# Two-layer graph network on 64 graphs: the layer-norm statistics of x, one pair of loads and the order of the first two graphs are moved

## What is computed

```python
h = relu(layernorm(x))                       # layer 0
q, k, v = h @ Wq.T + bq, h @ Wk.T + bk, h @ Wv.T + bv
w = adj * exp(q @ k.T)
x = x + (w / w.sum(axis=2)) @ v
h = relu(layernorm(x))                       # layer 1
A = adj + I; d = A.sum(-1) ** -0.5
x = x + (A * d[:, None] * d[None, :]) @ (h @ W + b)
```

## Time and profile before

| | us |
|---|---|
| median of 3 runs | 1716.59 (1712.29 to 1718.35) |
| the profiled execution | 1706.24 |
| its span, first to last instruction | 1704.4 |
| TensorE busy | 1640.7 (96%) |
| VectorE / ScalarE / GpSimd busy | 1475.4 / 1060.4 / 831.3 |

### The profile page before, as it was taken

How to read it: one execution, slowest core, us unless ns; L and a number is a source line. 1 busy time by engine, 2 the same in 40 slices (tenths; PEclk the granted TensorE clock), 3 DMA queues, 4 the chain that set the end, 5 groups by cost and what they waited for, 6 DMA issues and landing times.

```text
span 1704.4 us, 37784 instructions
## 1 busy us (share of the span) xinstructions
PE 1640.7 (96%) x12010; PEld 1551.3 (91%) x12010; DVE 1475.4 (87%) x3366; ACT 1060.4 (62%) x2451; POOL 831.3 (49%) x968
## 2 busy tenths in 40 slices
PE   8899999999999999999999999999999999999997
PEld 6798999999999999999998989999999999999996
DVE  5788888888888889888898889898888898888885
ACT  5656666666666666666666666666666666566552
POOL 2445445545545545545454554554554554454551
PEclk9899999999999999999999999999999999999998
DMA  5354554544544544544544544544544544545530
GB/s 171 83 146 116 124 136 118 131 132 114 139 130 118 137 126 122 137 123 121 142 122 112 148 117 117 149 120 116 151 117 117 149 120 116 146 117 122 145 100 28
DMA packets 494415, 212.66 MB, mean 125 GB/s; under 512 B 402496, under 2 KB 427072, under 8 KB 494400
## 3 DMA queue, kind: packets, MB, share of 16 engines
q1 hardware_dynamic: 492480, 210.89, 47.2%
q10 hardware_dynamic: 1920, 1.58, 0.3%
HBM read 146.28 MB, written 66.13 MB: 125 GB/s over the span
## 4 chain that ended last, share of the span: by engine, by line
DMA 28%; DVE 24%; issue 16%; SPq 14%; ACT 11%; PE 5%; POOL 1%; DVEq 0%; ACTq 0%; POOLq 0%
DMA x_in<-in_x_dram 15%; DMA h_scratch<-h 12%; SPq L185 10%; ACT unused_x L424 5%; ACT unused_x L431 5%; DVE z_lo L773 4%; DVE late L824 3%; DVE ht_lo L804 3%; DVE unused_a L793 3%; DVE p L784 3%; DVE p_lo L692 2%; DVE neg_mean L648 2%; SPq L223 2%; PE ps L836 2%; DVE v_lo L638 1%
## 5 line engine op out<-in xcount | busy, mean ns | idle before, releaser
L836 PE MATMUL ps<-ht_hi,m_hi 128*128 128x256 f32 x1024 | 287.2, 280 | 0.6 <-DVE m_lo L558 0.6
L838 PE MATMUL ps<-ht_lo,m_hi 128*128 128x256 f32 x1024 | 286.8, 280 | 0.0
L839 PE MATMUL ps<-ht_hi,m_lo 128*128 128x256 f32 x1024 | 286.4, 280 | 0.0
L408 ACT ACTIVATE g_hi<-ps,u_col 128x256 fp32r<-128x256 f32 x256 | 105.8, 464 | 251.8 <-PE ps L839 251.8
L284 POOL TENSOR_TENSOR ht_sum<-ht 128x256 f32<-128x256 f32 x64 | 47.4, 741 | 422.8 <-DVE ht L666 401.5
L836 PE MATMUL ps<-w_hi,z_hi 128*128 128x512 f32 x512 | 206.7, 404 | 38.1 <-DVE z_lo L773 38.1
L839 PE MATMUL ps<-w_hi,z_lo 128*128 128x512 f32 x512 | 202.0, 395 | 0.0
L838 PE MATMUL ps<-w_lo,z_hi 128*128 128x512 f32 x512 | 202.0, 394 | 0.0
L836 PEld LDWEIGHTS ps<-ht_hi,m_hi 128*128 128x128 f32 x1024 | 193.5, 189 | 0.7 <-DVE m_lo L558 0.7
L839 PEld LDWEIGHTS ps<-ht_hi,m_lo 128*128 128x128 f32 x1024 | 193.4, 189 | 0.0
L838 PEld LDWEIGHTS ps<-ht_lo,m_hi 128*128 128x128 f32 x1024 | 193.3, 189 | 0.0
(11 more groups left out here) (147 smaller groups left out, 5843.3 us busy)
## 6 DMA issues: line engine op xcount, KB each, us to landing
x_in<-in_x_dram SPq DMA_DIRECT2D x64, 512.0 KB, 4.3
xb<-in_x_dram SPq DMA_DIRECT2D x64, 512.0 KB, 4.9
out_dram<-late SPq DMA_DIRECT2D x128, 256.0 KB, 2.1
h_scratch<-h SPq DMA_DIRECT2D x62, 512.0 KB, 3.5
h_blocks<-h_scratch SPq DMA_DIRECT2D x248, 128.0 KB, 3.6
adj_in<-in_adj_dram SPq DMA_DIRECT2D x64, 256.0 KB, 2.9
adj_blocks<-in_adj_dram SPq DMA_DIRECT2D x256, 64.0 KB, 2.4
dn_row<-dn_scratch SPq DMA_DIRECT2D x64, 128.0 KB, 2.9
```

Source lines behind the costliest of these rows:

```text
L408: last = act.activation(g_hi[:, m, :], ps[:, G + j, m % 2 * N:m % 2 * N + N], ACT.Identity, bias=u_col[:, m:m + 1])
L836: pe.matmul(dst, a_hi[:, c, cols], b_hi[:, c, :], start=(first and c == 0), stop=False, skip_group_check=not first)
L838: pe.matmul(dst, a_hi[:, c, cols], b_lo[:, c, :], start=False, stop=False, skip_group_check=not first)
L839: end = pe.matmul(dst, a_lo[:, c, cols], b_hi[:, c, :], start=False, stop=(c == chunks - 1), skip_group_check=not first)
```

## The change

It moves work between places in the engines' orders; nothing of the computation is dropped.

- **Loop, statistics**: ACT runs `x_sums` between the two exponentials and `x_squares` after them. DVE runs `x_mean` between the two `p`, `x_variance` after the row sums of layer 1 and `x_shift` after `p_lo`. POOL's power for `rs_x` follows `ht_sum`.
- **Loop, rest**: SP loads `xb` ahead of `x_in`. POOL adds the bias to `xb` ahead of `ht_sum`, and makes `ht_sum_lo` ahead of `hat_lo`. On ACT `ht_sum_hi` and the adjacency's copy move behind `h` of the next step.
- **First two graphs**: `ht_lo` reads PSUM and not `ht`; the columns of `wt` come first and `values` waits for the parts of `wt_lo` one by one; the high and low part of W, the adjacency's copy and the statistics of graphs 2 and 3 move; TensorE waits for `ht_lo` where it waited for `ht`.

```diff
@@ sync: step
-                if second:
-                    x_second = x_flat[bass.ds(sp.snap((this + 1) * (N * D)), N * D)]
-                    if not prev:
-                        sp.wait_ge(h_ready[0], this + 1)
-                        sp.wait_ge(h_ready[1], this + 1)
-                    sp.dma_start(x_in[:], ...).then_inc(x_loaded, 16)
                 if main and prev:
                     ...
                     sp.dma_start(xb[:], ...).then_inc(xb_loaded, 16)
+                if second and prev:
+                    load_x(this)
...
+                if second and not prev:
+                    sp.wait_ge(h_ready[0], this + 1)
+                    sp.wait_ge(h_ready[1], this + 1)
+                    load_x(this)
@@ gpsimd: step
+                    if main:
+                        ht_sums_low(this)
                     pool.wait_ge(hat_hi_ready, this - 1)
...
-                    if main:
-                        ht_sums_low(this)
...
-                if main and ahead and prev:
-                    pool.wait_ge(v_done[V3], this)
-                    ht_sums(this + 1)
-                if second:
-                    pool.wait_ge(ve_x_done, this + 2)
-                    pool.tensor_tensor(rs_x[:], ve_x[:], minus_half[:], ALU.pow).then_inc(rs_x_done, 1)
                 if main:
                     ... (xb plus bias)
-                if main and ahead and not prev:
+                if main and not prev:
+                    x_power(this + 1)
+                if main and ahead:
                     pool.wait_ge(v_done[V3], this)
                     ht_sums(this + 1)
+                if second and main:
+                    x_power(this + 2)
@@ scalar: step
-                if main and ahead:
+                if main and ahead and prev:
                     layer_norm_x(this, prev, older)
+                if main and prev:
+                    ht_sums_high(this)
+                    keep_adjacency(this, True)
...
-                    if second:
-                        x_sums(this + 2)
+                    if not prev:
+                        x_sums(this + 1)
                     act.wait_ge(v_done[V2], this)
                     act.activation(v_hi[:, 0, 0, 0:HD], ps[:, VA, 0:HD], ACT.Copy).then_inc(v_hi_ready[0], 1)
-                    if second:
-                        x_squares(this + 2)
+                    if not prev:
+                        x_squares(this + 1)
...
                     for t in range(NT):
-                        if ahead and prev and t:
-                            ht_sums_high(this + 1)
+                        if t and not prev:
+                            layer_norm_x(this, prev, older)
+                        if t and second and prev:
+                            x_sums(this + 2)
                         ... (exponential t)
+                    if second and prev:
+                        x_squares(this + 2)
@@ vector: step
                     value_u3(this)
-                    if second:
-                        x_mean(this + 2)
                     value_sums(this)
                     value_low(this)
-                    if second:
-                        x_variance(this + 2)
...
-                    if second:
-                        x_shift(this + 2)
                     for t in range(NT):
+                        if t and second and prev:
+                            x_mean(this + 2)
                         ... (p of half t)
...
                 if main and prev:
+                    if second:
+                        x_variance(this + 2)
                     p_low(this)
+                    if second:
+                        x_shift(this + 2)
...
-                                          ht[:, 2 * j:2 * j + 2, :].rearrange("p c n -> p (c n)"),
+                                          ht[:, 2 * j:2 * j + 2, :].rearrange("p c n -> p (c n)") if prev
+                                          else ps[:, HT + j, :],
@@ tensor: values (weights_ready(2) to (8) in turn), step
-                weights_ready(8)
+                weights_ready(2)
                 value(V1, VA, ht_rows(0), upper, B11, HD + 2)
                 pe.wait_ge(ht_sum_lo_ready, 2 * this)
+                weights_ready(3)
                 value(V6, VB, sums(S2), whole, T2, HD + 2)
...
                         if ahead and not prev and t:
-                            pe.wait_ge(ht_ready[0], this + 1)
-                            pe.wait_ge(ht_ready[1], this + 1)
+                            pe.wait_ge(ht_lo_ready[0], this + 1)
+                            pe.wait_ge(ht_lo_ready[1], this + 1)
```

More of the change, by code:

```diff
@@ L217, in _, with load_x @@
             adj_flat, x_flat = adj.rearrange("g n m -> (g n m)"), x.rearrange("g n d -> (g n d)")
+            def load_x(this):
+                x_second = x_flat[bass.ds(sp.snap((this + 1) * (N * D)), N * D)]
+                sp.dma_start(x_in[:], x_second.rearrange("(t p d) -> p t d", p=P, d=D)).then_inc(x_loaded, 16)
             def step(this, prev, main, ahead, older=True, second=True):
@@ L433, in x_squares, with keep_adjacency @@
                 last.then_inc(x_square_ready, 1)
+            def keep_adjacency(graph, main=False):
+                act.wait_ge(adj_loaded, graph * 16)
+                if main:
+                    act.wait_ge(sd_ready, graph - 1)
+                for t in range(NT):
+                    last = act.activation(adj_kept[:, t, :], adj_in[:, t, :], ACT.Copy,
+                                          accum_out=rsum[:, t:t + 1])
+                last.then_inc(rsum_ready, 1)
             def hat_high(this):
@@ L473, in step @@
                     layer_norm_x(this, prev, older)
+                    keep_adjacency(this + 1)
                     for j in range(2):
@@ L482, in step @@
                     wt_high()
-                    x_sums(this + 2)
-                    x_squares(this + 2)
+                    w_high()
                 if prev:
@@ L514, in step @@
                                        ACT.Copy).then_inc(ht_hi_ready[j], 1)
[L515 to L524, removed]
                 if main and not prev:
-                    w_high()
+                    x_sums(this + 2)
+                    x_squares(this + 2)
             steps(act, step)
@@ L584, in wt_low @@
             def wt_low():
[L585 to L590, removed]
+                dve.wait_ge(wt_hi_ready, 1)
                 dve.tensor_tensor(wt_lo[:, B11:B21 + 1:2, :, HD:HD + 2], c_cols[:, 0:2],
@@ L594, in wt_low @@
                                   wt_hi[:, T2:T4 + 1, :, HD:HD + 2].bitcast(fp32), ALU.subtract).then_inc(wt_lo_ready, 1)
+                dve.wait_ge(t_ready, 4)
+                for k, block in enumerate((B11, T2, T1, T4, B21, T3, B22)):
+                    dve.wait_ge(wt_hi_ready, k + 2)
+                    dve.tensor_tensor(wt_lo[:, block, :, 0:HD], wt[:, block, :, 0:HD],
+                                      wt_hi[:, block, :, 0:HD].bitcast(fp32), ALU.subtract).then_inc(wt_lo_ready, 1)
             def w_low():
@@ L758, in step @@
                         dve.tensor_copy(wt[:, B11:B11 + 2, c, 0:HD], halves(ps[:, WV_BANKS[c], :])).then_inc(wvt_kept[0], 1)
-                    dve.wait_ge(wvt_kept[0], 2)
-                    dve.tensor_tensor(wt[:, T1, :, 0:HD], wt[:, T3, :, 0:HD], wt[:, B11, :, 0:HD],
-                                      ALU.subtract).then_inc(t_ready, 1)
                 if main:
+                    if not prev:
+                        x_mean(this + 1)
                     value_u3(this)
-                    if second:
-                        x_mean(this + 2)
                     value_sums(this)
                     value_low(this)
-                    if second:
-                        x_variance(this + 2)
+                    if not prev:
+                        x_variance(this + 1)
                 if prev:
```

32 lines of the change are left out of this document (21 added, 11 removed).

## The result

The changed kernel takes 1665.1 us (median of 4 runs, 1656.7 to 1668.0), beside 1714.4 us for the kernel before on the same chip: a ratio of 0.9707, interval 0.9659 to 0.9755. Its profiled execution fell from 1706.24 to 1666.89 us.

What follows compares the result with a forecast made beforehand. TensorE, busy in nearly every slice, was taken to lose 0.79 us a step waiting for `z_lo`, behind `x_in` and the statistics. 1706.24 − 34.8 (loop) − 5 (start) = 1666.4, plus 10.35 to the median: 1677 us, range 1655 to 1704.

Steps and rivals of the forecast that it cites:

- 1670 to 1690: Whole kernel: the narrower band in us around the forecast of 1677, given a chance of 0.45.
- The wait of 0.79 us a step goes, and some 0.2 come back: Loop: TensorE's wait for `z_lo` goes; 0.1 us lost to POOL, 0.1 to late graphs; 34.8 us gained over 59 steps.
- POOL's addition holds L629 and L638: DVE in the loop: POOL's `xb` addition delays these two instructions by 0.8 and some 0.3 us.
- a shortage of spare between S and W in one graph: TensorE in the loop: POOL's holds take 1.1 us of 1.0 us spare ahead of W, so 0.1 us is lost.
- The row sums with 0.4 us of spare: Loop: adjacency's row sums come about 7.8 us behind W, SP wants them at 8.2; later would delay `h_blocks` and transposes.
- Rival C: Loop: `h_blocks` arrives later by the 0.8 us won, so nothing changes: 1712 or 1716 us; chance 0.06.
- Other moves at nothing: Loop: the other moves on ACT, SP and POOL, including the new load order, cost nothing as spare covers them.
- rival D: Loop: statistics between the exponentials make `p_hi`, `p_lo` and `h` late; 1748 us; chance 0.08, shared with worst `xb` landing.
- The first graphs, 5 us: Start: half of TensorE's four long waits, 10.5 us together, goes: 5 us gained, bounds 0 and 10.5.
- 10.35 us from the profile to the median: Whole kernel: median of the runs, 1716.59, lies 10.35 us above the profiled 1706.24; added to the forecast.
- The range: Whole kernel: 1655 to 1704 us, leaving out the no-change and slower cases.
- rival A: Loop: the whole wait for `z_lo` goes as DVE mostly slips between POOL's additions; 1665 us; chance 0.22.

Runs made afterwards that it cites:

- stats_only: Kernel before, with only the loop's statistics of x moved on ACT and DVE and POOL's power behind its `xb` addition: ratio 0.9768 to the kernel before.
- stats_back: Changed kernel with only the loop's statistics of x put back in their old place on ACT and DVE: 79 us slower than the kernel before.
- before_store_first: Kernel before, with only SP's store of `h` issued ahead of the next adjacency's load: ratio 0.9706 to the kernel before.
- no_xb_add: Changed kernel with POOL's bias addition to `xb` left out but for one element: ratio 0.9642 to the kernel before.
- z_first: Changed kernel with DVE making `z_lo` ahead of two sums of v: 10 us more than the changed kernel measured again on the same chip.
- sp_back_store_first: Changed kernel with `x_in` loaded ahead of `xb` again and the store of `h` ahead of the next adjacency's load: ratio 0.9641 to the kernel before.
- The second execution: Changed kernel measured and profiled once more, nothing altered: ratio 0.9690 to the kernel before.
- store_first: Changed kernel with SP's store of `h` issued ahead of the next adjacency's load: ratio 0.9646 to the kernel before.
- pool_back: Changed kernel with POOL's `ht_sum` ahead of `xb` in the loop again: 9 us more than the changed kernel measured again on the same chip.
- sp_back: Changed kernel with SP loading `x_in` ahead of `xb` again: ratio 1.0015 to the kernel before.

## Why the prediction came out as it did

Forecast 1677, measured 1665: faster, inside the range, 12 us under the forecast and outside its own 1670 to 1690. By its steps:

- *The wait of 0.79 us a step goes, and some 0.2 come back.* The step fell by 0.63, forecast 0.59: 37.3 us, forecast 34.8. Right, and stats_only and stats_back show that it was the statistics' move that gave it; before_store_first shows that it was not the only way.
- *POOL's addition holds L629 and L638.* Forecast 0.8 and 0.3 us; in the graph shown 0.97 and 0.08, in the mean over the loop 0.7 and 0.3. Right. By no_xb_add the step pays 0.22 us for the addition. The booked 0.2 had the right size, though half of it was booked for late graphs and the way from the hold to the step was another (next point), so its size is partly luck.
- *Where the rest comes from.* The forecast took the residual as a shortage of spare between S and W in one graph. That is the step that was incomplete. z_first put `z_lo` ahead of what POOL holds and gained nothing; sp_back_store_first left POOL's hold as long as it was and the wait was gone. What is left is a ring that carries every delay into the next step.
- *The row sums with 0.4 us of spare.* SP's load of the adjacency was issued 7.87 us behind W (forecast 7.8), the store of `h` at 8.56. Rival C named this member as the next in line and priced only that it might come later; its sign, more waits of the transposes for `h_blocks`, did come (44 for 27), its time did not. The opposite move was the lever: with the store first `h_blocks` is issued 1.2 us earlier in the kernel before (11.26 for 12.44 us behind W), and that was worth the whole change.
- *Other moves at nothing.* `x_in` made ACT wait for no DMA, and the loop has no wait for `p_lo`: rival D did not occur. The new order of the loads is no free move, though: beside POOL's new order it is worth 1.0015 − 0.969, some 56 us by ratios on two chips, 38 to 39 us by the profiled executions.
- *The first graphs, 5 us.* W of step 2 came at 76.73 in place of 81.69, 5.0 us earlier; at step 3 W waited 3.04 us and 1.7 were left. The second execution left 4.6 at step 3, and there all three terms fit: 35.2 for the loop, 4.6 for the start, 0.7 for the end. So the first one does not show the term wrong, only that it stopped at step 2 and left out a wait that follows. Ahead of this wait, from the store of `h` to the issue of `h_blocks`, it took 4.96 us (86.41 to 91.37) and 5.09 in the second execution, 3.5 in the loop; why is not shown. With store_first W of step 3 has no wait and comes at 98.09.
- *10.35 us from the profile to the median.* The sum in the profile's own terms was 1666.4 and the profiled execution took 1666.89. That the sum is met to half a us is luck in part: in this execution the loop gave 2.5 us more and the start 3.3 less than forecast. The median of the changed kernel is 1.8 us below its profile, where that of before was 10.35 above; carrying this distance over made nearly the whole miss of 12 us. Whether it belonged to that one execution or to its chip stays open: 1706.24 lies below all runs of the kernel before in the result (1708.3 to 1718.4), but amid those on the chip where it takes 1707 us.
- *The range.* Its lower end does not follow from its terms: the whole wait and the whole start gained give 1706.24 − 46.7 − 10.5 + 10.35 = 1659, not 1655. The measured time is above both.

The time is that of rival A, the mechanism is not: A wanted DVE not to be held.

How much of the start's gain is real with the loop of before stays open, between 0 and 3 us. Whether a place for POOL's addition exists that holds nobody was not found; with the store first none is needed.

## What to carry to other kernels

In a pipelined loop, follow the chain of waits over a whole round before pricing one wait in it, even where the rounds are independent: engines that work strictly in order can close a ring. If DMA, SP and "issue" hold much of the chain and the busiest engine little, suspect one. It is a sign and no proof: before_store_first had the same 5% for TensorE with hardly a wait left. What shows it is a run that takes time out at a place of which no wait of TensorE speaks, here two issues on one queue. Reordering within the ring (pool_back, z_first) gained nothing. And price a profiled execution against a profiled execution on the same chip: the distance of one to a median did not carry over from kernel to kernel.

## What the runs showed of the hardware

- POOL's addition held DVE's instructions with two inputs in SBUF at each place where it was put: v22 1.38 us for 0.41, the bias row 1.78 for 0.75. DVE held POOL too: POOL's L295 took 1.19 us in sp_back (797.50), the same sum in the kernel before (L287) 0.74.
- An instruction with one input in SBUF was held too. In sp_back `neg_mean`, 2 elements a row, took 0.70 us from 798.89 and ended with POOL's L297 (798.76 + 0.80); alone it takes 0.16. The Trainium skill (SBUF — State Buffer, § Who interferes with whom) says that such a scalar operation can enter a two-port mode in which it contends with GpSimd. The trace agrees that it is held, with 699 ns in the mean; the mode itself no trace shows. The prediction gave the rule on a single input without this exception, and took the 0.58 us of `neg_mean` in the earlier trace rows as its own time: it ended at 848.31, POOL's L287 at 847.54 + 0.74 = 848.28.
- The store of `h` took 3.5 us from its issue to that of `h_blocks` with the adjacency's load issued 0.7 us ahead of it, and 3.0 us with that load behind it, in both kernels (medians over the loop).
